# One matrix per system in place of attention and inverse, by factors per row stored with the systems

## The chip, the cores and the metric

The kernel runs on one core of one Trainium2 chip, in fp32. The metric is the device time of one execution in microseconds. Before the change it is 774.7 us, the median of 3 runs (774.45 to 776.15).

## The reference

A small vision tower over 64 images of 96 x 96: patch embedding to 37 tokens of width 256 per image, a first layer (multi-query attention and a mixture by entmax gates), a second layer, then 8 experts with top-1 routing. The change is in the second layer's attention, a gated delta rule. An image has 37 tokens, fewer than one chunk of 64, so the state stays zero and what remains is, per image and head (2 heads of 128):

```python
k = x / max(norm(x), 1e-12)                    # x: normalised rows, one head
v = (x @ W_write.T) * beta;  beta = sigmoid(x @ W_beta.T)
A0 = tril(-(k*beta) @ k.T * L, -1)             # L[i, j] = gamma ** (i - j)
A = solve_triangular(eye - A0, eye, lower=True, unit_diagonal=True)
attn = tril(k @ k.T * L)
o = attn @ (A @ v)
out = rows + o @ W_read.T                      # both heads side by side
logits = layernorm(out) @ Wr + br              # of the experts' router
```

## The kernel before, in words

The 64 images are worked three at a time: a tile is 111 rows (R = 111, 3 images of 37 tokens), 22 tiles (NT) in 11 pairs (PAIRS). The phase in question is one block of five programs that run beside each other and meet in semaphores; each engine takes its own instructions strictly in the order written.

**Steady loop** (`for i in range(-1, PAIRS + 2)`, about 303 to 447 us). Pair i goes through the first layer's mixture (first_products, gate_first, hidden, second_products, gate_second, outputs on TensorE, ScalarE and VectorE). Pair i-1 is normalised (add_outputs, power_rows on GpSimd, normalise, turn_rows). Pair i-2 gets its values and Gram matrices (row_products: x @ W_write, W_beta and k k^T per head in banks 6 and 7); decay_products on VectorE multiplies the Gram bank by two masks, giving the transposed attention attn_t (kept in memory for all tiles) and the system nf. On GpSimd strengths makes beta times the inverse norms, fold brings the three images' columns of a tile together, 37 wide, times strength. GpSimd's order in turn i is strengths(i-2, 0), fold(i-2, 0), power_rows(i-1), strengths(i-2, 1), add_rows(i-1), fold(i-2, 1); at i = PAIRS the spreads of tiles 0 and 1 follow.

**Systems.** SP stores them to n_rows in device memory and loads them with one system (37 x 37) per partition, in three groups: pairs 0 to 4, 5 to 7 and 8 to 10 (GROUPS). With fewer systems than partitions the columns of the inverse are split over 2, 3 or 4 sets. substitution(g) on VectorE solves two rows per step: one product of two SBUF operands (line 1750) and one reduction (line 1757) per part. It is a generator: between the other duties of a turn advance(budget) runs steps up to a budget by estimated cost (SLOTS). The inverse goes by SP through a_rows and comes back as rows (store_inverses, load_inverses). SP's order is: systems of groups 0, 1; inverses of group 0; systems of group 2; inverses of group 1; the 8 MB load of the experts' W1 (line 1350); inverses of group 2; half of W2; the token rows of all 22 tiles (line 1357).

**Read loop** (`for t in range(2, NT + 5)`, to about 526 us), per tile: spread_inverses (GpSimd, line 1898) makes the block matrix of the inverse times beta; solve_values (TensorE, 1457), copy_solved (ScalarE, 1583), attend (1468), copy_attended (1590), read_out with each head in its own half bank (1478). The first head is scaled by its inverse norm on ScalarE (scale_first, 1605) and added on GpSimd (add_first, 1930), the second head scaled and added on VectorE (add_read, 1784) ahead of statistics (1788), aggregate (1790) and variance (1792); power_outputs on GpSimd (1909, 1910), normalise_outputs on ScalarE (1612), turn_outputs (1491), copy_turned (1597), router_logits (1500), keep_logits on VectorE (1798, with the bias). advance continues the substitution; before tile 10 group 1 has to be finished, before tile 16 group 2. Then come the routing (route) and the experts.

The last turn of the steady loop holds the first tiles of the read loop: on TensorE

```python
if i == PAIRS + 1:
    solve_values(0)
row_products(i - 2, 0)
...
if i == PAIRS + 1:
    attend(0)
    solve_values(1)
row_products(i - 2, 1)
```

## Time and profile before

| what | us |
|---|---|
| median of 3 runs (lowest, highest) | 774.7 (774.45, 776.15) |
| the profiled execution | 774.87 |
| its span, first to last instruction | 773.1 |
| busy: TensorE, VectorE, GpSimd, ScalarE | 691.6, 419.6, 292.1, 246.4 |
| mean granted TensorE clock, of full speed | 0.945 |
| embedding and first attention | 0 to 268 |
| gates by entmax | 268 to 303 |
| steady loop | 303 to 447 |
| read loop, up to the last logits | 447 to 526 |
| routing | 526 to 553 |
| experts | 553 to 773 |

A time in a row is the time from the start of the span. Busy time of TensorE says how long matrix products were in its pipeline; their ends are modelled, so the steps of a turn are read from start to start. What an engine waited for stands in square brackets behind its idle time. Where VectorE or TensorE is busy for a whole window, no wait of theirs decides; where none is, the last one's releaser does.

### The profile page before, as it was taken

The numbers are of one execution on the slowest core, as the hardware profiler recorded it, in microseconds if no ns is written. First come the engines' busy times: TensorE is split into PE (matmuls) and PEld (weight loads), VectorE is DVE, ScalarE is ACT, GpSimd is POOL, SyncE is SP. The second block draws the span as 40 slices with busy tenths as digits, with TensorE's granted clock in tenths as the row PEclk, the third lists the DMA queues.
The fourth block names the chain that finished last, engine by engine and source line by source line (L and its number), as shares of the span: only waits on it lengthen the run. The fifth ranks groups of instructions, "written<-read, shape, count | busy, mean of one in ns | idle before, by whom it ended". The sixth has DMA issues, their size and how long they took to land.

```text
span 773.1 us, 13815 instructions
## 1 busy us (share of the span) xinstructions
PE 691.6 (89%) x4632; PEld 518.9 (67%) x4632; DVE 419.6 (54%) x1120; ACT 246.4 (32%) x679; POOL 292.1 (38%) x483
## 2 busy tenths in 40 slices
PE   5899999999997689999999689497999999999994
PEld 3567776676765445999998567374667676766763
DVE  2466677777665466334389999457233323333331
ACT  0122333333333114344444246261122223232231
POOL 2334454544444100255576687360222322222221
PEclk9899999999998779999999899796799999999998
DMA  8311001111100000000101327598211111111110
GB/s 292 137 37 37 20 25 31 37 37 37 37 1 2 1 1 2 1 8 6 40 8 36 41 44 290 210 361 306 56 40 43 49 54 47 58 42 56 47 35 14
DMA packets 25070, 50.73 MB, mean 66 GB/s; under 512 B 15611, under 2 KB 15741, under 8 KB 24363
## 3 DMA queue, kind: packets, MB, share of 16 engines
q1 hardware_dynamic: 21387, 35.36, 14.4%
q0 software_dynamic: 3328, 10.23, 4.4%
q10 hardware_dynamic: 288, 4.27, 1.4%
q8 instruction: 39, 0.64, 0.4%
q14 instruction: 28, 0.23, 0.1%
HBM read 39.99 MB, written 9.86 MB: 64 GB/s over the span
## 4 chain that ended last, share of the span: by engine, by line
PE 45%; DVE 7%; issue 4%; POOL 3%; ACT 0%; POOLq 0%; DVEq 0%; ACTq 0%
PE psum L1199 12%; PE psum L1175 12%; PE psum L1396 4%; PE psum L1408 4%; PE psum L1188 3%; PE psum L1442 2%; DVE work L1750 2%; PE psum L1376 1%; DVE arena_w L1757 1%; PE psum L1386 1%; PE psum L1018 1%; PE psum L1418 1%; POOL work L1909 1%; PE psum L1448 1%; POOL work L1898 1%
## 5 line engine op out<-in xcount | busy, mean ns | idle before, releaser
L1272 ACT ACTIVATE work<-psum,cst 128x128 f32<-128x128 f32 x208 | 56.5, 383 | 144.2 <-PE psum L1188 144.2
L1175 PE MATMUL psum<-arena_w,work 128*128 x208 | 93.7, 593 | 1.0 <-DVE work L1226 1.0
L1199 PE MATMUL psum<-arena_w,work 128*128 x416 | 94.2, 379 | 0.4 <-ACT work L1272 0.4
L1137 POOL DMA_INDIRECT out<-work,row_i x26 | 25.7, 988 | 158.2 <-DVE work L1248 158.2
L1199 PEld LDWEIGHTS psum<-arena_w,work 128*128 128x128 f32 x416 | 77.1, 190 | 10.5 <-issue 1.1
L1235 DVE COPY work<-psum 128x512 f32<-128x512 f32 x52 | 36.0, 692 | 67.5 <-PE psum L1175 67.5
L347 PE MATMUL psum<-arena_w 128*111 128x256 f32 x264 | 63.3, 392 | 4.9 <-DMA arena_w<-in_pack 4.9
L712 POOL TENSOR_TENSOR arena_w<-arena_w,work 101x592 f32<-101x592 f32 x33 | 39.5, 1198 | 71.6 <-DVE work L578 71.6
L1175 PEld LDWEIGHTS psum<-arena_w,work 128*128 128x128 f32 x208 | 37.5, 190 | 38.6 <-issue 38.6
L347 PEld LDWEIGHTS psum<-arena_w 128*111 128x111 f32 x264 | 46.1, 181 | 19.2 <-issue 9.6
L703 POOL TENSOR_TENSOR arena_w<-arena_w 128x296 f32<-128x296 f32 x66 | 44.0, 689 | 21.2 <-DVE arena_w L546 21.2
L1242 DVE TENSOR_TENSOR tokens<-psum,cst 128x256 f32<-128x256 f32 x26 | 11.1, 425 | 73.9 <-PE psum L1199 73.9
L401 PE MATMUL psum<-arena_w 128*37 128x296 f32 x264 | 41.5, 436 | 3.3 <-ACT arena_w L666 3.3
L635 ACT COPY arena_w<-psum 37x592 f32<-37x592 f32 x33 | 25.2, 763 | 57.8 <-PE psum L412 57.8
L558 DVE TENSOR_REDUCE work<-psum 101x16 f32<-101x592 f32 x33 | 25.4, 770 | 24.0 <-PE psum L401 24.0
L1130 POOL DMA_INDIRECT tokens<-x_rows,row_i x26 | 25.4, 978 | 33.1 <-DVE gate_s L1093 25.5
L1396 PE MATMUL psum<-arena_w 128*128 128x222 f32 x176 | 37.6, 357 | 0.0
L412 PEld LDWEIGHTS psum<-cst,arena_w 101*128 101x128 f32 x264 | 26.1, 148 | 16.7 <-POOL arena_w L712 8.6
L433 PE MATMUL psum<-arena_w 37*32 37x74 f32 x1056 | 24.9, 232 | 13.5 <-DVE arena_w L569 12.2
L433 PEld LDWEIGHTS psum<-arena_w 37*32 37x32 f32 x1056 | 19.5, 108 | 24.3 <-issue 24.3
L627 ACT ACTIVATE arena_w<-arena_w 101x592 f32<-101x592 f32 x33 | 23.5, 711 | 37.4 <-DVE arena_w L561 36.4
L1408 PE MATMUL psum<-arena_w 128*128 128x222 f32 x176 | 35.2, 352 | 0.0
(224 smaller groups left out, 1377.6 us busy)
## 6 DMA issues: line engine op xcount, KB each, us to landing
arena_w<-in_w SPq DMA_DIRECT2D x2, 4096.0 KB, 12.7
arena_w<-in_x SPq DMA_DIRECT2D x22, 333.0 KB, 2.9
x_rows<-tokens SPq DMA_DIRECT2D x22, 192.0 KB, 4.0
arena_w<-in_pack ACTq DMA_DIRECT2D x1, 2442.0 KB, 10.8
cst<-in_packc ACTq DMA_DIRECT2D x1, 1727.0 KB, 14.8
arena_w<-in_pack SPq DMA_DIRECT2D x1, 818.5 KB, 7.1
arena_w<-in_pack SPq DMA_DIRECT2D x2, 384.0 KB, 4.3
arena_w<-n_rows SPq DMA_DIRECT2D x8, 85.6 KB, 3.1
```

The costliest lines, as they stand in the source:

```text
L347: mm = nc.tensor.matmul(bank[0][0:R, j * D:(j + 1) * D], xp[j][:, k * R:(k + 1) * R], w_lin[:, k, :], start=(k == 0), stop=(k == PC - 1))
L401: mm = nc.tensor.matmul(bank[4 + f][e * HP:e * HP + TOK, 0:HH * TOK], qt[:, a:a + TOK], kb[p % 2 * 2 + e], start=True, stop=True)
L412: mm = nc.tensor.transpose(turns_bank[:, c * 128:c * 128 + PR], prob[p % 2][:, c * 128:(c + 1) * 128], ident[0:PR, 0:PR])
L433: mm = nc.tensor.matmul(out[32 * b:32 * (b + 1)], vpad[i % 2][:, v0:v0 + 2 * HD], probs[:, :, r0:r0 + TOK], start=(e == 0), stop=(e == 1))
L703: nc.gpsimd.tensor_tensor(kb[p % 2 * 2 + e].rearrange("p (h s) -> p h s", h=HH), kt[:, a:a + TOK].unsqueeze(1).broadcast_to([128, HH, TOK] ...
L712: nc.gpsimd.tensor_tensor(by_head(prob[p % 2], HP), by_head(prob[p % 2], HP), small[p % 2][:, 2 * NH:3 * NH].unsqueeze(2).broadcast_to([PR ...
L1175: mm = nc.tensor.matmul(bank[2 * j + f][:, :], xgt[j][:, k * 128:(k + 1) * 128], arena_w1[:, bass.ds(expert * (2 * FF) + (k * FF + f * 512 ...
L1199: mm = nc.tensor.matmul(bank[7][:, 0:D], ht[j][:, g * 128:(g + 1) * 128], arena_w2[:, bass.ds(expert * (FC * D) + g * D, D)], start=(g == ...
L1235: nc.vector.tensor_copy(hp[j][:, f * 512:(f + 1) * 512], bank[2 * j + f][:, :]).then_inc(h_out[j], 1)
L1272: nc.scalar.activation(ht[j][:, g * 128:(g + 1) * 128], bank[4 + f][:, k * 128:(k + 1) * 128], ACT.Gelu, bias=cst[:, bass.ds(expert * FC + ...
L1396: mm = nc.tensor.matmul(bank[2 + f // 2 % 2][:, (f % 2) * W:(f % 2 + 1) * W], w_out1[:, f, :], z1, start=True, stop=True)
L1408: mm = nc.tensor.matmul(bank[1][:, 0:W], w_in2[:, f, :], hid[:, f * W:(f + 1) * W], start=(f == 0), stop=(f == OC - 1))
```

## The change

One matrix per system takes the place of two. Row i of attn is row i of (M - 1) over beta plus attn's own diagonal, so attn @ A is the inverse with a factor per row plus a diagonal of 1/beta. attn_t, its mask, its product on TensorE and the copy between are dropped. Each row of a system is stored with two more numbers (NW = 39 in place of 37 columns): the diagonal's share and the row's factor. At the end of substitution(g) the solved columns are multiplied by the row's scale, and the diagonal's share (own, one product on GpSimd, own_factors) is added: three more VectorE operations per group in place of none. factors(i) on VectorE makes the two numbers for a pair, a reciprocal and a fused operation on four elements per partition, behind GpSimd's strengths.

Both heads now have the right scale before read_out, which sums them in one bank (bank 2 + t%2): scale_first and add_first are dropped and add_read is one plain addition. The `EPS` addition of the variance goes from VectorE to GpSimd, keep_logits to ScalarE without the bias, which route adds once for all tiles. strengths handles a pair at a time; GpSimd's order becomes power_rows, strengths, fold, fold, add_rows. identity_columns of all groups move into turns 0 to 2 of the steady loop, and the systems of all groups have places of their own. On TensorE the read loop's order becomes attend(t), turn_outputs(t-5), read_out(t-1), router_logits(t-5); on ScalarE copy_attended, copy_turned, normalise_outputs, keep_logits. The diff, cut:

```diff
+NW = TOK + 2
...
+                link(tt(by_tile(lgr), by_tile(lgr), c("b_r", R).unsqueeze(1).broadcast_to([R, NT, NE]), ALU.add))
...
+                    sp.wait_ge(factors_ready, 2 * (t // 2 + 1))
...
-                def solve_values(t):
-                    if not tile(t):
-                        return
-                    pe.wait_ge(a_block, t + 1)
-                    free(pe, vn_out, t - 1)
-                    for h in range(H1):
-                        mm = nc.tensor.matmul(bank[t % 2][0:R, h * 128:(h + 1) * 128], ab[t % 2][:, h * R:(h + 1) * R],
-                                              x_half(t)[:, h * 128:(h + 1) * 128], start=True, stop=True)
-                    mm.then_inc(vn_done, 1)
-
                 def attend(t):
                     if not tile(t):
                         return
-                    pe.wait_ge(vn_out, t + 1)
+                    pe.wait_ge(a_block, t + 1)
                     free(pe, o_out, t - 1)
                     for h in range(H1):
-                        a = (t * H1 + h) * R
-                        mm = nc.tensor.matmul(bank[2 + t % 2][:, h * R:(h + 1) * R], vn[t % 2][:, h * 128:(h + 1) * 128],
-                                              attn_t[:, a:a + R], start=True, stop=True)
+                        mm = nc.tensor.matmul(bank[t % 2][:, h * R:(h + 1) * R], x_half(t)[:, h * 128:(h + 1) * 128],
+                                              ab[t % 2][:, h * R:(h + 1) * R], start=True, stop=True)
                     mm.then_inc(o_done, 1)
 
...
-                        mm = nc.tensor.matmul(bank[4 + t % 2][0:R, h * D:(h + 1) * D], ot[t % 2][:, h * R:(h + 1) * R],
-                                              w_read[:, h, :], start=True, stop=True)
+                        mm = nc.tensor.matmul(bank[2 + t % 2][0:R, 0:D], ot[t % 2][:, h * R:(h + 1) * R],
+                                              w_read[:, h, :], start=(h == 0), stop=(h == H1 - 1))
...
                     if i == PAIRS + 1:
-                        solve_values(0)
+                        attend(0)
                     row_products(i - 2, 0)
                     outputs(i - 1)
                     hidden(i, range(OC // 2))
                     if i == PAIRS + 1:
-                        attend(0)
-                        solve_values(1)
+                        attend(1)
+                        read_out(0)
                     row_products(i - 2, 1)
                     gates(i + 1)
                     hidden(i, range(OC // 2, OC))
                     turn_rows(i - 1)
-                pe.wait_ge(y_added, PAIRS)
-                read_out(0)
-                attend(1)
                 for t in range(2, NT + 5):
-                    solve_values(t)
+                    attend(t)
+                    turn_outputs(t - 5)
                     read_out(t - 1)
-                    turn_outputs(t - 5)
-                    attend(t)
                     router_logits(t - 5)
                 route_products(pe)
                 expert_products(pe)
@@ -1575,35 +1553,25 @@
                                          scale=0.5).then_inc(beta_out, 1)
                     nc.scalar.copy(x_half(t), bank[6][0:R, 0:D]).then_inc(v_out, 1)
 
...
                 for t in range(2, NT + 5):
+                    copy_attended(t)
+                    copy_turned(t - 5)
                     normalise_outputs(t - 4)
-                    copy_solved(t)
-                    copy_turned(t - 5)
-                    scale_first(t - 1)
-                    copy_attended(t)
+                    keep_logits(t - 5)
...
-                    nc.vector.tensor_tensor(attn_t[:, t * H1 * R:(t + 1) * H1 * R], bank[7][0:R, 0:H1 * R], lt, ALU.mult)
...
-                    nc.vector.engine_nop().then_inc(solved[g], 1)
+                    nc.vector.tensor_tensor(x, x, n[:, :, TOK + 1].unsqueeze(1).broadcast_to([used, cols, TOK]),
+                                            ALU.mult).then_inc(scaled[g], 1)
+                    dve.wait_ge(scaled[g], 1)
+                    dve.wait_ge(factored[g], 1)
+                    band = rows_x[0:used, 0:(cols - 1) * (TOK + sets)].rearrange("p (c i) -> p c i", c=cols - 1)[:, :, 0:sets]
+                    nc.vector.tensor_tensor(band, band, own[0:used, 0:TOK - 1].rearrange("p (c k) -> p c k", k=sets),
+                                            ALU.add).then_inc(solved[g], 1)
+                    corner = rows_x[0:used, cols * TOK - 1:cols * TOK]
+                    nc.vector.tensor_tensor(corner, corner, own[0:used, TOK - 1:TOK], ALU.add).then_inc(solved[g], 1)
...
-                    dve.wait_ge(inverted, t // 2 + 1)
-                    dve.wait_ge(half_added, t + 1)
-                    nc.vector.scalar_tensor_tensor(h, bank[4 + j][0:R, D:2 * D], inv_all[:, t * H1 + 1:t * H1 + 2], h,
-                                                   ALU.mult, ALU.add).then_inc(added, 1)
+                    dve.wait_ge(summed, t // 2 + 1)
+                    nc.vector.tensor_tensor(h, h, bank[2 + j][0:R, 0:D], ALU.add).then_inc(added, 1)
...
+                def factors(i):
+
+                    if not pair_of(i):
+                        return
+                    cols = slice(2 * H1 * i, 2 * H1 * (i + 1))
+                    b0 = 2 * i % NB
+                    to = nk_all.rearrange("p (b h n) -> p b h n", b=NB, h=H1)[:, b0:b0 + 2]
+                    dve.wait_ge(strong, i + 1)
+                    dve.wait_ge(inv_out, i + 1)
+                    for b in (b0, b0 + 1):
+                        free(dve, n_stored[b], 16 * len(ROW_CUTS) * (2 * i // NB))
+                    nc.vector.reciprocal(to[:, :, :, TOK], beta[:, cols].rearrange("p (b h) -> p b h", b=2)
+                                         ).then_inc(factors_ready, 1)
+                    dve.wait_ge(factors_ready, 2 * i + 1)
+                    nc.vector.scalar_tensor_tensor(to[:, :, :, TOK + 1], sn[:, cols].rearrange("p (b h) -> p b h", b=2), 0.5,
+                                                   to[:, :, :, TOK], ALU.mult, ALU.subtract).then_inc(factors_ready, 1)
...
+                def strengths(i):
+
+                    if not pair_of(i):
+                        return
+                    cols = slice(2 * H1 * i, 2 * H1 * (i + 1))
+                    pool.wait_ge(inverted, i + 1)
+                    pool.wait_ge(beta_out, 2 * i + 2)
+                    link(ts(beta[:, cols], th[:, cols], 1.0, 2e-9, ALU.add, ALU.max))
+                    tt(beta[:, cols], beta[:, cols], inv_all[:, cols], ALU.mult).then_inc(strong, 1)
+                    pool.wait_ge(strong, i + 1)
                     link(tt(strength[:, cols], beta[:, cols], inv_all[:, cols], ALU.mult))
-                    tt(beta_img[:, t * H1 * IPT:(t + 1) * H1 * IPT].rearrange("p (h m) -> p h m", m=IPT),
-                       beta[:, cols].unsqueeze(2).broadcast_to([R, H1, IPT]),
-                       c("mask_img", R).unsqueeze(1).broadcast_to([R, H1, IPT]), ALU.mult).then_inc(beta_masked, 1)
+                    tt(beta_img[:, cols.start * IPT:cols.stop * IPT].rearrange("p (h m) -> p h m", m=IPT),
+                       beta[:, cols].unsqueeze(2).broadcast_to([R, 2 * H1, IPT]),
...
+                def own_factors(g):
+
+                    used = group_of(g)[3] * SETS[g]
+                    pool.wait_ge(zeroed[g], 3)
+                    pool.wait_ge(n_in[g], 16 * H1 * SETS[g])
+                    tt(solve_at[g][3][0:used, :], solve_at[g][2][0:used, :],
+                       solve_at[g][0][0:used, :].rearrange("p (i j) -> p i j", i=TOK)[:, :, TOK], ALU.mult).then_inc(factored[g], 1)
...
-                    pool.wait_ge(vare2, t + 1)
+                    pool.wait_ge(aggr2, t + 1)
                     free(pool, normed2, t - 1)
+                    link(ts(ve2[t % 2][:, 0:1], st2[t % 2][:, 7:8], EPS, None, ALU.add))
...
-                    strengths(i - 2, 0)
+                    power_rows(i - 1)
+                    strengths(i - 2)
                     fold(i - 2, 0)
-                    power_rows(i - 1)
-                    strengths(i - 2, 1)
+                    fold(i - 2, 1)
                     add_rows(i - 1)
-                    fold(i - 2, 1)
                     if i == PAIRS:
                         spread_inverses(0)
                         spread_inverses(1)
                     inverses(i - 1)
-
-                def add_first(t):
-                    if not tile(t):
-                        return
-                    pool.wait_ge(half_out, t + 1)
-                    pool.wait_ge(summed, t // 2 + 1)
-                    tt(h_rows(t), h_rows(t), first_half[t % 2], ALU.add).then_inc(half_added, 1)
-
+                    if i - 3 in ends:
+                        own_factors(ends[i - 3])
                 for t in range(NT + 2):
-                    add_first(t - 1)
                     spread_inverses(t + 2)
                     power_outputs(t - 2)
+                    if t == 4:
+                        own_factors(LAST)
                 send_and_gather(pool)
 
 
@@ -1990,9 +1979,7 @@
```

## Rows read from the trace of the kernel before

**Rows 1.** Windows: us, busy of TensorE, weight loads, VectorE, ScalarE, GpSimd; clock, DMA, GB/s

```profile
397.00:409.00 12.00, 12.00 (x67) 11.00 (x66) 11.54 (x37) 5.15 (x18) 7.71 (x20) 1.00 0.03 5
418.50:440.00 21.50, 14.27 (x80) 12.24 (x78) 20.56 (x55) 6.13 (x22) 14.27 (x34) 0.98 0.27 48
...
470.00:487.00 17.00, 16.85 (x116) 14.27 (x116) 16.24 (x69) 11.79 (x33) 13.72 (x25) 1.00 1.00 410
487.00:500.00 13.00, 2.08 (x15) 1.67 (x14) 4.87 (x17) 1.16 (x4) 0.86 (x2) 0.75 0.43 144
```

**Rows 2.** Timeline of SP's queue: start us, us, engine, line, operation, out<-in, count

```profile
470.66 0.36 SPq L1350 DMA_DIRECT2D arena_w<-in_w  x1
492.13 3.68 SPq L1325 DMA_DIRECT2D a_rows<-arena_w  x8
497.15 2.66 SPq L1331 DMA_DIRECT2D arena_w<-a_rows  x6
...
500.28 27.38 SPq L1357 DMA_DIRECT2D x_rows<-tokens  x44
```

**Rows 3.** Timeline of GpSimd at tile 16

```profile
499.14 0.56 POOL L1898 TENSOR_TENSOR work<-arena_w 111x222 f32<-111x222 f32 x1 [12.39 <-DMA arena_w<-a_rows]
```

**Rows 4.** Timeline of TensorE, one read turn

```profile
506.63 0.67 PE L1457 MATMUL psum<-tokens,work 111*111 111x128 f32 x4
507.14 1.03 PE L1478 MATMUL psum<-cst,work 128*111 128x256 f32 x4
...
508.20 0.61 PE L1468 MATMUL psum<-arena_w,work 111*128 111x111 f32 x4
508.80 0.56 PE L1500 MATMUL psum<-cst,work 128*111 128x8 f32 x4
```

**Rows 5.** Timeline of VectorE, the last tile's first mask

```profile
447.30 0.39 DVE L1696 TENSOR_TENSOR arena_w<-psum,arena_w 111x222 f32<-111x222 f32 x1 [1.23 <-PE psum L1448]
```

**Rows 6.** Timeline of VectorE in the routing

```profile
529.29 0.29 DVE L1046 RECIPROCAL work<-work 111x22 f32<-111x22 f32 x1
```

**Rows 7.** Timeline of VectorE, identity columns of the last group

```profile
443.15 0.53 DVE L1707 TENSOR_TENSOR arena_w<-cst,arena_w 128x370 f32<-128x370 f32 x1
```

**Rows 8.** Timeline of GpSimd, turn PAIRS of the steady loop

```profile
436.84 0.20 POOL L1872 TENSOR_SCALAR arena_w<-arena_w 111x2 f32<-111x2 f32 x1
...
437.95 1.09 POOL L1855 TENSOR_TENSOR tokens<-tokens,arena_w 111x512 f32<-111x512 f32 x1
...
440.12 0.56 POOL L1898 TENSOR_TENSOR work<-arena_w 111x222 f32<-111x222 f32 x1
```

**Rows 9.** Timeline of TensorE, start of the steady loop's last turn

```profile
440.73 1.19 PE L1457 MATMUL psum<-tokens,work 111*111 111x128 f32 x4 [2.42 <-POOL work L1898]
```

**Rows 10.** Timeline of VectorE, one read turn

```profile
464.27 0.48 DVE L1784 SCALAR_TENSOR_TENSOR tokens<-psum,arena_w,tokens 111x256 f32<-111x256 f32 x1
...
465.25 0.18 DVE L1790 BATCH_NORM_AGGREGATE work<-work 111x2 f32<-111x6 f32 x1
465.47 0.15 DVE L1792 TENSOR_SCALAR work<-work 111x1 f32<-111x1 f32 x1
465.54 0.16 DVE L1798 TENSOR_TENSOR work<-psum,cst 111x8 f32<-111x8 f32 x1
```

**Rows 11.** Groups of 303 to 531 us: busy us, mean ns of one | idle before, releaser

```profile
L1930 POOL TENSOR_TENSOR tokens<-tokens,work 111x256 f32<-111x256 f32 x22 | 14.3, 648 | 8.8 <-ACT work L1605 8.7
...
L1909 POOL TENSOR_TENSOR work<-work 111x1 f32<-111x1 f32 x22 | 14.1, 641 | 4.1 <-DVE work L1792 4.1
```

**Rows 12.** Windows of line 1750, then of line 1757: VectorE busy, clock, DMA, GB/s

```profile
462.00:492.00 30.00, 8.36 (x29) 1.00 0.76 294
...
462.00:492.00 30.00, 7.32 (x29) 1.00 0.76 294
```

**Rows 13.** DMA issues of 499 to 516 us: count, KB each, median us to landing

```profile
x_rows<-tokens SPq DMA_DIRECT2D x11, 192.0 KB, 11.1
```

**Rows 14.** Timeline of TensorE in the drain

```profile
520.11 0.56 PE L1500 MATMUL psum<-cst,work 128*111 128x8 f32 x4 [0.43 <-ACT work L1597]
```

More of the change, by code:

```diff
@@ L146, in build @@
         lg0 = carve_1b(NT * E0, R)
+        carve_2 = carver(arena_w1)
+        for g in range(1, len(GROUPS) - 1):
+            solve_at[g] = [carve_2(w) for w in (TOK * NW, TOK * COLS[g], TOK, TOK)]
         zeros = arena_w2[:, W2S - RW // 2:W2S]
@@ L922, in build @@
             ab = [wc(H1 * R, R) for _ in range(2)]
-            vn = [wc(D, R) for _ in range(2)]
             ot = [wc(H1 * R) for _ in range(2)]
@@ L927, in build @@
             halves = wc(4, R)
-            first_half = [wc(D, R) for _ in range(2)]
-            ac = arena_w2[0:R, W2S // 2 + NT * H1 * R:W2S // 2 + NT * H1 * (R + TOK)]
             def pair_of(i):
@@ L1812, in _ @@
                     decay_products(i - 2, 1)
+                    factors(i - 2)
                     if i - 3 in ends:
```

141 lines of the change are left out of this document (56 added, 85 removed).

## The prediction

> **What bounds the kernel now.** I read the windows by stage first [rows 1]. Up to 418 us TensorE is the bound: from 397 to 409 it is busy 12.00 of 12.00 us, VectorE 11.54. From there to 492 us VectorE is: 20.56 of 21.50 us, later 16.24 of 17.00. Between 487 and 500 nobody is: TensorE works 2.08 of 13 us. The experts behind 553 us are TensorE's, and the change doesn't touch them. So it can act in three places: the turn of the pipeline into the read loop (418 to 450 us), the read turns beside the substitution (450 to 492), and the last turns with the routing (500 to 553).
>
> Then the timelines, for what ends each. When VectorE has solved the last group of systems, SP issues its stores at 492.13 and its loads at 497.15 [rows 2]; GpSimd spreads tile 16 at 499.14, after 12.39 us idle that a DMA ended [rows 3]. That chain sets when the last six tiles can start. Behind it a turn takes 2.57 us, and TensorE fills it [rows 4].
>
> **The change, part by part. The steady loop (to 418 us): nothing.** VectorE loses one mask of two per tile (0.39 us alone [rows 5], about 0.3 from start to start) and gains two four-element factor operations per pair. No four-element reciprocal is in the trace: the 22-element one takes 0.29 us [rows 6], the smallest vector operations 0.15, and the second waits for the first. So a pair of factors costs 0.3 to 0.6 us; I take 0.45, towards the reciprocal's row. Minus 0.60 plus 0.45 a pair is covered by a TensorE without a gap; should the factors' wait hold VectorE (11.54 of 12.00 here), each 0.1 us over the 0.46 left is a gap on TensorE in each of some three turns. The exponentials and products dropped ahead of the loop, and the identity columns moved into its first turns, where VectorE is far from full, count zero too.
>
> **The end of the first group (430 us): +1.05.** A substitution gets three operations at its end. A product of 370 elements takes 0.53 us [rows 7], one of 222 the 0.39 of rows 5: a slope of 0.95 ns per element, so the scalings of 703, 481 and 370 elements cost about 0.86, 0.64 and 0.53 us, the band and corner additions 0.15 to 0.20 each. With waits 1.2, 0.95 and 0.85 us. GpSimd's factor product is ready long before. The first 1.2 stands in front of gate_second of the last pair, for which TensorE's outputs wait; the dropped masks and new factors give 0.15 back. Queued behind it on VectorE is the whole last pair.
>
> **The turn into the read loop: +1.35 more.** GpSimd's order changes. Before, strengths and fold of the first tile stand ahead of power_rows; the second tile's strengths start at 436.84, the row addition at 437.95, and with a fold between tile 0's spread starts at 440.12 [rows 8]. After, the strengths (1.1 us, as from 436.84 to 437.95), both folds (1.15 each) and the addition (1.05) all follow power_rows, which ends at about 437.5: 437.5 + 1.1 + 2.3 + 1.1 = 442.0. TensorE waits for this spread ahead of the last pair's row products: it waited 2.42 us, to 440.73 [rows 9], and now waits to about 442.7. In front of the second tile's products stands now a read_out as well (0.87 us, 1.4 while the clock is low), and a product set fewer. The last tile's mask, at 447.30 after a 1.23 us wait for TensorE [rows 5], comes at about 449.6, and the factors behind it wait for strengths that need the same tile's values: another 0.3. The last group's identity columns (0.53) no longer lie in the way, but VectorE waits there anyway. In all the first read addition comes +2.4 us (bounds +0.5, if GpSimd catches up, and +4).
>
> **The read turns on VectorE: -4.0.** One turn is in [rows 10]: the fused read addition takes 0.48 us at 464.27, aggregate 465.25, variance 465.47, logits 465.54. The plain addition of 256 elements should take 0.42 to 0.43 by the mask's 0.39 for 222: 0.05 saved. The variance operation, now GpSimd's, saves 0.19 with its wait, the logits copy, now ScalarE's, 0.07. That is 0.24 in each of 14 turns and 0.07 in nine of them: 4.0. The ends of groups 1 and 2 take 0.95 and 0.85. So the last group is solved at +2.4 - 4.0 + 1.8 = +0.2 us. GpSimd also loses its addition of 0.65 us per turn [rows 11]. The substitution's product (two SBUF inputs) and reduction (one) of equal size take 8.36 and 7.32 us in 462 to 492 [rows 12]: 1.0 us goes there beside a working GpSimd, of which I give back 0.3.
>
> The Trainium skill (SBUF — State Buffer, Who interferes with whom) has it that a VectorE instruction with two SBUF inputs and a GpSimd one that reads SBUF exclude each other. This trace agrees in that only the two-input form is longer; by the page each new scaling, two-input itself, could also be held by one GpSimd operation.
>
> **The queue is a floor.** Group 1 is solved about 2.4 us later too, so the 8 MB weight load, issued at 470.66 [rows 2], goes at about 473. At the 410 GB/s of the window 470 to 487 [rows 1] it takes 20 us: to 493 instead of 491. The last group's stores stand behind it on the same queue: token stores behind the next weight load landed 11 us after their issue [rows 13], which is what such a place costs. Eight stores take 3.68 us to issue, so behind 493 they land at about 497, as now. Solving the last group sooner gains nothing below that. I take 0 for all up to the spread of tile 16, bounds -1 and +2.
>
> The Trainium skill (DMA: Bandwidth & Descriptors, Queues, rings and completion order) says each DMA engine takes a ring's descriptors in order; that would be this floor's reason.
>
> **The last turns: -4.0.** TensorE's turn, by starts: solve 0.51, read and transposes 1.06, attend with the wait for ScalarE's copy 0.60, logits 0.41 [rows 4]. After: attend alone 0.44 (0.51 times 111/128 columns), 1.06, now covering the copy, and 0.41: 1.91. GpSimd's turn is the spread 0.56, an added operation 0.27, the power 0.64 and its follower 0.27 [rows 3, 8, 11]: 1.74, just below. Six turns: -4.0. The turn with the last read has no solve; there the covered copy saves 0.6. In the four turns of drain (logits wait 0.43 for the copy [rows 14], 1.24 a turn at the high clock) the normalisation (0.6) now stands behind that copy and ahead of the next transposes: 1.5 in place of 1.24 in two or three, +0.6. The token stores take 27.4 us of SP from 500.28 [rows 2]; they can end no later than now, and the routing's need for them comes some 8 us after the last logits.
>
> **Routing: +0.4.** The bias is added in one linked operation of 176 elements (0.35, between 0.15 and the mask's 0.39) behind the last logits.
>
> **Sum.** 0.0 - 4.0 + 0.4 = -3.6 on the profiled execution's 774.87 (span 773.1): 771.2. The runs' median, 774.7, is 0.2 lower, less than the terms are good for.
>
> **Rivals.** (A) The turn costs nothing net: GpSimd, with fewer operations per pair, is ahead there, the spread comes by 441 us, and the weight load moves forward with the substitution. For it: GpSimd's row shows no long idle time to lose. Against it: both folds now stand ahead of the spread. Price: VectorE's -2.2 come through, -6: 769. Chance 0.17.
> (B) The last turns don't reach 1.91 us because GpSimd's turn with its waits, or the round over the engines, is 2.25. For it: 1.74 against 1.91 is close. The gain there halves: -1.6, 773.3. Chance 0.15.
> (C) Slower. Tile 0's spread, and TensorE's last row products with it, come later than I say. Each microsecond past 442 delays the last pair's systems, VectorE and the weight load alike: from 445.6 the gain is gone, at 447.5 it is +1.8: 776.7. For it: these are stores and loads of short rows through memory, whose issue moves 1 us. Against it: the spread followed GpSimd's work without idle time, so the loads had landed. Chance 0.09.
> (D) It does not do what it says: the removed chain (solve, copy, second scaling) was hidden, and the two sides cancel: 774.7. It holds for the 14 turns that are VectorE's, not for the last six. Chance 0.04.
>
> **How the numbers follow.** Forecast 0.55 (own range 769.7 to 772.9), A 0.17, B 0.15, C 0.09, D 0.04. The range takes in most of A, B and D: 767.8 to 774.8. A measurement here tells about 0.2%, 1.55 us: faster are the forecast, A and a third of B, less the forecast's upper end, 0.75; same two thirds of B, D and some of the forecast, 0.16; slower C, 0.09.
>
> **What would show it.** Right: tile 0's spread near 442; SP's stores of the last group within 1 us of 492.13 and the 8 MB load near 473; turns of 1.9 us behind tile 16's spread. Wrong: gaps on TensorE before 418 behind factors that wait for strengths; GpSimd full in the last turns; tile 16's spread over 2 us from 499.14.

## The result, and the profile after

The changed kernel takes 780.6 us (median of 7 runs, 777.8 to 783.4) against 774.9 of the kernel before: a ratio of 1.0074 with a 95% interval of 1.0051 to 1.0096. I had predicted 771.2, within 767.8 to 774.8. It is slower, and outside the range. The profiled execution took 782.11 us, its span 780.2 (before: 774.87 and 773.1).

First the sections of the span. The steady loop doesn't start at the same time in every profile (the copy that ends the part ahead of it starts between 300.5 and 303.3 us, in kernels of both kinds alike), so all marks below count from that copy, which is the same in both kernels.

| us from that copy | before | after | difference | forecast of the difference |
|---|---|---|---|---|
| the copy itself, from the span's start | 301.49 | 302.95 | +1.46 | 0 |
| stores of group 0's inverses | 128.56 | 130.70 | +2.14 | +1.05 |
| stores of group 1's inverses | 160.91 | 164.82 | +3.91 | |
| issue of the 8 MB of weights | 169.17 | 173.01 | +3.84 | +2.4 |
| stores of the last group's inverses | 190.64 | 191.37 | +0.73 | +0.2 |
| their loads | 195.66 | 198.44 | +2.78 | 0 |
| last logits on TensorE | 223.84 | 228.20 | +4.36 | -4.0 |
| end of the span | 471.61 | 477.25 | +5.64 | -3.6 |

SP's queue after (answers to [rows 2]: start, us, engine, line, operation, count):

```profile
433.65 2.09 SPq L1317 DMA_DIRECT2D a_rows<-arena_w  x4
...
467.77 2.41 SPq L1317 DMA_DIRECT2D a_rows<-arena_w  x6
...
475.96 0.36 SPq L1343 DMA_DIRECT2D arena_w<-in_w  x1
494.32 3.71 SPq L1317 DMA_DIRECT2D a_rows<-arena_w  x8
501.39 2.66 SPq L1323 DMA_DIRECT2D arena_w<-a_rows  x6
```

TensorE in the last turns after (answers to [rows 4]; L1450 is the one product set that is left, L1460 the read):

```profile
488.70 0.47 PE L1482 MATMUL psum<-cst,work 128*111 128x8 f32 x4
504.10 1.20 PE L1450 MATMUL psum<-work,tokens 111*128 111x111 f32 x4 [14.93 <-POOL work L1891]
505.09 0.58 PE L1473 MATMUL psum<-cst,tokens 111*128 111x111 f32 x2
505.46 1.91 PE L1460 MATMUL psum<-cst,work 128*111 128x256 f32 x4
507.17 0.78 PE L1482 MATMUL psum<-cst,work 128*111 128x8 f32 x4
507.80 1.18 PE L1450 MATMUL psum<-work,tokens 111*128 111x111 f32 x4
```

A turn is 3.70 us here and 3.68 in each of the four that follow, where before took 2.57. Yet TensorE has less to do and no gap: most operations take nearly twice their time (the read 1.91 us against 1.03 in rows 4). The clock column goes with it, the third from the right, 0.50 being the lower level, 1.2 GHz, and 1.00 the 2.4 GHz. Windows of before:

```profile
492.00:498.00 6.00, 0.00 (x0) 0.00 (x0) 0.00 (x0) 0.00 (x0) 0.00 (x0) 0.63 0.20 29
...
506.00:510.00 4.00, 4.00 (x31) 3.43 (x30) 1.61 (x7) 3.19 (x10) 2.73 (x6) 1.00 0.94 393
```

and of after:

```profile
506.00:510.00 4.00, 4.00 (x17) 3.42 (x16) 1.14 (x4) 1.67 (x6) 3.14 (x8) 0.50 0.94 401
510.00:516.00 6.00, 6.00 (x25) 5.30 (x24) 2.06 (x6) 1.74 (x6) 2.65 (x7) 0.50 0.95 350
516.00:522.00 6.00, 6.00 (x24) 5.07 (x23) 1.03 (x3) 2.54 (x7) 2.10 (x6) 0.50 0.98 366
522.00:526.00 4.00, 4.00 (x30) 3.67 (x29) 2.31 (x7) 2.26 (x7) 1.71 (x6) 0.92 0.98 346
```

Both kernels fall to half clock in the stall before tile 16. Before is back at full when the second turn starts, 4.3 us after TensorE resumed; after gets it back 18.5 us after, when five of the six turns are over. At full clock the changed turn takes 1.89 us (475.05 to 476.94, before the stall), and 1.91 was forecast:

```profile
475.05 0.68 PE L1450 MATMUL psum<-work,tokens 111*128 111x111 f32 x4
...
476.94 0.68 PE L1450 MATMUL psum<-work,tokens 111*128 111x111 f32 x4
```

The second thing to see is the end of group 0 (VectorE and GpSimd, interleaved by start; L1733 is the scaling, L1738 the band, L1741 the corner, L1837 GpSimd's row addition; the last line is TensorE's first work behind it, which waited 3.40 us for VectorE's gate_second, where it had waited 1.40 before):

```profile
430.77 1.60 DVE L1733 TENSOR_TENSOR arena_w<-arena_w 120x703 f32<-120x703 f32 x1
431.01 2.49 POOL L1837 TENSOR_TENSOR tokens<-tokens,arena_w 111x512 f32<-111x512 f32 x1
432.40 1.16 DVE L1738 TENSOR_TENSOR arena_w<-arena_w 120x36 f32<-120x36 f32 x1
433.48 0.15 DVE L1741 TENSOR_TENSOR arena_w<-arena_w 120x1 f32<-120x1 f32 x1
...
435.97 1.12 PE L1411 MATMUL psum<-arena_w 128*111 128x256 f32 x4 [3.40 <-DVE arena_w L1623]
```

The scaling takes 1.60 us for the 0.86 of my sum, the band 1.16 for 0.20, and GpSimd's addition 2.49 for the 1.09 of [rows 8].

### The profile page after: what moved, and what is told of

Read it like the earlier page. It is cut to its first block, busy times and chain, and to the rows that moved or that the text cites. A ratio compares the mean times of both kernels' runs of the same rounds, so it can differ in the third digit from the quotient of the medians.

```text
span 780.2 us, 13524 instructions
## 1 busy us (share of the span) xinstructions
PE 689.9 (88%) x4544; PEld 518.4 (66%) x4544; DVE 414.2 (53%) x1092; ACT 234.0 (30%) x655; POOL 283.9 (36%) x451
## 4 chain that ended last, share of the span: by engine, by line
PE 48%; DVE 5%; issue 4%; POOL 2%; DMA 0%; ACT 0%; DVEq 0%; POOLq 0%; ACTq 0%
PE psum L1192 12%; PE psum L1168 11%; PE psum L1389 4%; PE psum L1401 4%; PE psum L1181 3%; PE psum L1435 2%; PE psum L1460 2%; PE psum L1369 1%; PE psum L1450 1%; PE psum L1010 1%; PE psum L1379 1%; DVE work L1720 1%; PE psum L1411 1%; PE psum L1441 1%; PE psum L1482 1%
## 5 line engine op out<-in xcount | busy, mean ns | idle before, releaser
L1450 PE MATMUL psum<-work,tokens 111*128 111x111 f32 x88 | 19.0, 352 | 22.8 <-POOL work L1891 22.8
L562 DVE TENSOR_REDUCE work<-psum 101x16 f32<-101x592 f32 x33 | 25.4, 771 | 24.1 <-PE psum L405 24.1
## 6 DMA issues: line engine op xcount, KB each, us to landing
arena_w<-in_w SPq DMA_DIRECT2D x2, 4096.0 KB, 12.7
```

The lines of the kernel that those rows point to most:

```text
L1450: mm = nc.tensor.matmul(bank[t % 2][:, h * R:(h + 1) * R], x_half(t)[:, h * 128:(h + 1) * 128], ab[t % 2][:, h * R:(h + 1) * R], start=Tru ...
```

## Experiments on the clock

Theory 1: the half clock in the last turns, which the long stall brings, costs the time. Rival: the turns are long by a chain of waits. A dummy is a product whose result nobody reads; it only gives TensorE work.

**Dummies in the stall.** Ahead of tile 16, on the changed kernel (fill_start(pe, 16) issues 16 products of 512 columns):

```diff
+                    if t == 16:
+                        pe.wait_ge(v_out, NT)
+                        pe.wait_ge(n_masked, NT)
+                        fill_start(pe, 16)
                     attend(t)
```

> The changed kernel, with 16 dummy matmuls of 512 columns put on TensorE ahead of tile 16's spread row products (into two banks that are free there), so that TensorE works in a part of the 14.93 us in which it stood before tile 16. Theory 1 (the clock: after the long stall the last six turns ran at half clock, 3.68 us each against 1.89 at full clock): the last turns fall to 1.9 to 2.6 us each, and the time falls by 6 to 9 us, to 772 to 775. Theory 2 (the last turns are long by their own chain of waits, and the low clock only goes along with it): the turns stay near 3.7 us and the time stays at 780.6 within 1 us, or rises by what the dummies delay.

Measured: 774.27 us, ratio 0.9988 (0.9976 to 1.0), 6.6 us by the ratios below the changed kernel. The dummies keep the clock at 1.00 through the stall, and the turns take 1.89 to 1.91:

```profile
486.25 13.98 PE L995 MATMUL psum<-cst 128*128 128x512 f32 x32
501.13 0.70 PE L1451 MATMUL psum<-work,tokens 111*128 111x111 f32 x4 [0.90 <-POOL work L1896]
...
503.04 0.68 PE L1451 MATMUL psum<-work,tokens 111*128 111x111 f32 x4
```

From the last group's loads to the last logits it takes 21.05 us instead of 29.76. Of these 8.7 us 1.6 are given back behind the last logits, in the routing. Theory 1 stands.

**The same on the kernel before** (11 dummies of 512 columns, in banks 0 and 2):

> The kernel before with 11 dummy matmuls of 512 columns on TensorE in its stall before tile 16, as the changed kernel got them. In the kernel before TensorE resumed at 499.7 and the granted clock was back at full by 504.1, so only the first two of its last turns were slow. Theory 1 (the clock sets the last turns only where it is low): tile 16's turn is 1 to 2 us shorter, the four after it keep their 2.57 us, and the time falls by 1 to 2.5 us, to 773 to 774. If the steady turns of before also shorten, the clock was at work in them too and the time falls by 3 or more.

774.38 us, 0.9990 (0.9978 to 1.0002). Loads to last logits 26.33 us instead of 28.18, the first turn 2.63 for 4.31, the others still 2.57. So the clock cost before 1.85 us there and after 8.7. With dummies in both, the two kernels are level (0.9988 and 0.9990): the changed one is 5.3 us shorter in the last turns, but its loads come 2.4 us later and it takes 1.6 us more behind the last logits. By these profiles 1.3 us would remain, which the runs don't show.

**A longer stall in the kernel before** (a memset and four linked 512-column products on GpSimd ahead of tile 16's spread):

> The kernel before, with one memset and four chained 512-column products put on GpSimd ahead of tile 16's spread, which lengthens TensorE's stall there from 10.9 us to about 14 to 16. Theory 1 with the clock decided by the length of the stall: the last turns, 2.57 us in the kernel before, run at half clock and take over 3 us, and the time rises by clearly more than the stall: by 7 to 10 us, to 782 to 785. If the stall only delays what follows: the time rises by the delay alone, 3 to 5 us, to 778 to 780.

785.63 us, 1.0129 (1.0098 to 1.016). TensorE stood 16.10 us, 5.2 more than before, and the last logits came 8.7 later: besides the delay itself, the first three turns took 4.55, 4.53 and 4.13 us in place of 4.31, 2.57 and 2.57. The old kernel can be held at half clock too; late in the third turn the clock was back, 12.7 us after the work resumed. The other 1.5 us of the profile came behind the last logits.

**Idle time or work?** Both could explain 18.5 us against 4.3: the changed kernel stands 4 us longer, and its turns hold less work. One kernel has only 4 dummies, at the start of the stall, which leaves TensorE 11.11 us idle; the other has none there, but one of 512 columns in each of the turns 16 to 18:

```diff
                     turn_outputs(t - 5)
+                    if 16 <= t <= 18:
+                        pe.wait_ge(v_out, NT)
+                        pe.wait_ge(n_masked, NT)
+                        fill_start(pe, 1)
```

> The changed kernel with only 4 dummies of 512 columns at the start of the stall (3.4 us at full clock), which leaves TensorE idle for some 11.5 us before tile 16, about as long as in the kernel before (10.91 us), where the clock was back 4.3 us after the work resumed. If the length of the idle time decides how long the clock stays low afterwards: it is back about 4 us after the resumption, one or two turns at 3.68 and the others at 1.89, and the time is 773 to 776. If it doesn't (the smaller work in a turn of the changed kernel keeps it low): five or six turns at 3.68 and 777 to 781.

> The changed kernel with its stall as it was (no dummies there) and one dummy of 512 columns in each of the turns 16, 17 and 18, so that a turn holds more of TensorE's work, as it did in the kernel before (whose clock came back 4.3 us after the work resumed). If too little work in a turn keeps the clock low: it is back within 4 to 8 us of the resumption, and the later turns take 1.89; the time is 775 to 779. If the stall alone decides: the clock stays at half for about 18 us as in the changed kernel, three turns are 1.7 us longer each, and the time is 783 to 787.

The four dummies bring nothing: 781.86 us, 1.0084 (1.0059 to 1.011), a little above the range of either expectation. The three in the turns bring nearly all: 774.76 us, 0.9999 (0.9986 to 1.0012). With 11.11 us idle and the plain turns (windows of that kernel):

```profile
510.00:516.00 6.00, 6.00 (x26) 5.49 (x25) 2.06 (x6) 1.93 (x7) 2.59 (x7) 0.50 0.93 335
516.00:522.00 6.00, 6.00 (x23) 5.07 (x23) 1.67 (x5) 2.23 (x7) 2.34 (x7) 0.50 1.05 392
```

With 14.65 us idle and a dummy in each of three turns:

```profile
506.00:510.00 4.00, 4.00 (x18) 2.96 (x17) 1.03 (x3) 1.22 (x4) 2.20 (x6) 0.74 1.13 483
510.00:516.00 6.00, 6.00 (x41) 5.02 (x40) 2.49 (x8) 2.71 (x10) 3.43 (x9) 1.00 0.85 288
```

TensorE is busy without a gap in both. In the kernel with a dummy a turn its first two dummies (L994) and the second and third turn read:

```profile
504.33 1.94 PE L994 MATMUL psum<-cst 128*128 128x512 f32 x2
...
508.23 0.68 PE L1450 MATMUL psum<-work,tokens 111*128 111x111 f32 x4
...
508.93 1.04 PE L994 MATMUL psum<-cst 128*128 128x512 f32 x2
...
511.00 0.68 PE L1450 MATMUL psum<-work,tokens 111*128 111x111 f32 x4
```

A dummy costs 1.7 us at half clock, and the clock was back 5 us after the work resumed, before the second one started. The second turn, dummy and all, takes 2.77 us, where the plain turn takes 3.68 at half clock; the turns behind the dummies take 1.89.

So here more work in the first turn brought the clock back (5 us for 18.5), and a shorter idle time (11.11 for 14.93 us) did not. That the work which the change took out would have done the same is argued, from the 4.3 us of the kernel before, and not shown: the same old turns, behind 16.10 us idle, were at half clock for 12.7 us. Whether the moment of the first dummy matters beside its work was not tested either.

## Experiments on the solving and the queue

**Without the finishing operations** (with the 16 dummies in the stall, as in all kernels from here on that build on the changed one; the inverses stay unfinished, so this one leaves a part of the work out):

```diff
-                    nc.vector.tensor_tensor(x, x, n[:, :, TOK + 1].unsqueeze(1).broadcast_to([used, cols, TOK]),
-                                            ALU.mult).then_inc(scaled[g], 1)
...
-                    nc.vector.tensor_tensor(band, band, own[0:used, 0:TOK - 1].rearrange("p (c k) -> p c k", k=sets),
-                                            ALU.add).then_inc(solved[g], 1)
...
-                    nc.vector.tensor_tensor(corner, corner, own[0:used, TOK - 1:TOK], ALU.add).then_inc(solved[g], 1)
+                    nc.vector.engine_nop().then_inc(solved[g], 2)
```

> As the changed kernel with the 16 dummies, and the three finishing operations of VectorE on a group's systems (the scaling by the column factors, the band and the corner added) left out, so the stored systems are unfinished: part of the computation is missing. My forecast priced the three at 1.05, 0.95 and 0.85 us at the ends of groups 0, 1 and 2. If they cost what the trace after suggests (the scaling 1.60 us, the band 1.16 and the chain behind them late by 2.0), group 0's and group 1's parts of the chain end about 2 us earlier each, and the time is 2.5 to 4 us below the kernel with dummies alone. If the queue of transfers (8 MB of weights, then the last group's stores and loads) sets the start of the last turns, group 1's end is hidden in part and the time falls by 2 us or less.

770.16 us, 0.9950 (0.9931 to 0.9969): 2.9 us by the ratios below the kernel with dummies alone. By the marks group 0's stores come 2.75 us sooner, group 1's 3.28, the last group's 4.09, but its loads only 3.25. The three operations cost at group 0 2.75 us where I had 1.2; the end of the first group is therefore mis-sized, and the two others add 0.5 and 0.8, where I had 0.95 and 0.85.

**Dense factors.** GpSimd copies the factor of each row into a dense tile beforehand, the scaling reads that:

```diff
-                    nc.vector.tensor_tensor(x, x, n[:, :, TOK + 1].unsqueeze(1).broadcast_to([used, cols, TOK]),
+                    nc.vector.tensor_tensor(x, x, factor[g][0:used, :].unsqueeze(1).broadcast_to([used, cols, TOK]),
```

> The changed kernel with the 16 dummies, and the scaling's second operand, the factors that lie one in each row of 39, copied into a dense tile of 37 by GpSimd beforehand (one small operation a group). The scaling took 0.83 us for 370 columns, 1.40 for 481 and 1.60 for 703, 2.2 to 2.9 ns a column, against 1.2 for the products beside it. If the stride of the operand makes it slow: 0.45 to 0.5, 0.6 to 1.1 and 0.85 to 1.1 us, and the time falls by 0.8 to 1.5 us. If it is GpSimd beside it or the broadcast: durations as they were, and no change within 0.5 us.

The scalings fall from 1.60, 1.15 and 0.84 us (with dummies alone) to 1.04, 0.66 and 0.55:

```profile
430.17 1.04 DVE L1740 TENSOR_TENSOR arena_w<-arena_w,work 120x703 f32<-120x703 f32 x1
431.25 1.15 DVE L1744 TENSOR_TENSOR arena_w<-arena_w 120x36 f32<-120x36 f32 x1
...
492.15 0.55 DVE L1740 TENSOR_TENSOR arena_w<-arena_w,work 128x370 f32<-128x370 f32 x1
```

So the reading with a stride cost a third and more, and 0.55 for 370 elements is close to the 0.53 of [rows 7]. The band stays at 1.15 us: it ended at 432.40, GpSimd's row addition at 432.33. The time doesn't move, 0.9990 (0.9978 to 1.0002); the last group's stores come 0.4 us sooner, its loads 25.28 us behind the weights, as ever.

**The queue.** From the issue of the 8 MB to the last group's loads it is 25.43 us after, 25.33, 25.39 and 25.28 in the three kernels with dummies so far, whatever the solve does, and 26.49 before. First I tried ScalarE's queue for the 8 MB, in its read turn 10:

> The changed kernel with the 16 dummies, and the 8 MB load of the first expert weights issued from ScalarE's queue as soon as group 1's inverses are stored, instead of from SyncE's queue behind group 1's loads (issue at 473.09 in the kernel with dummies). If the queue's order (weights, then the last group's stores and loads behind them) sets the start of tile 16, which my forecast took for hidden and the trace after puts at 2 us, the last group's stores land and its inverses are back 1.5 to 3 us earlier, and the time falls by 1.5 to 3 us below the kernel with dummies alone (ratio 0.995 to 0.997). If the engines share the bandwidth so that the last group's stores wait all the same: within 0.5 us of it.

785.69 us, 1.0132 (1.0112 to 1.0153). The load was issued at 478.06, 2.2 us later by the marks than with the dummies alone, since ScalarE reached the place only then (its copy at 477.84 stands just ahead). The last group's stores were issued from 495.14 on, while the weights still came in (312 GB/s from 495 to 499), and took 8.52 us to issue for 3.71:

```profile
495.14 8.52 SPq L1318 DMA_DIRECT2D a_rows<-arena_w  x8
505.00 2.65 SPq L1324 DMA_DIRECT2D arena_w<-a_rows  x6
```

Why the issue itself was slow is not shown; from 499 to 503.7 the DMA engines were only 0.19 busy. The 16 dummies ended 3.93 us before tile 16's first products, and the clock was lost again: all six turns behind it take about 3.7 us. So this run mixes two losses and says nothing on the order itself. The next does: SP's own order, with 6 MB ahead of the last group and the second weights behind the rows' stores:

```diff
-                sp.dma_start(arena_w1[:, :], w1_h).then_inc(w1_in, 16)
+                sp.dma_start(arena_w1[:, 0:W1A], w1_h[:, 0:W1A]).then_inc(w1_in, 16)
                 store_inverses(LAST)
                 load_inverses(LAST)
-                sp.dma_start(arena_w2[:, 0:W2S // 2], w2_h[:, 0:W2S // 2]).then_inc(w2a_in, 16)
+                sp.dma_start(arena_w1[:, W1A:W1S], w1_h[:, W1A:W1S]).then_inc(w1_in, 16)
                 for t in range(NT):
...
+                sp.dma_start(arena_w2[:, 0:W2S // 2], w2_h[:, 0:W2S // 2]).then_inc(w2a_in, 16)
                 sp.wait_ge(x_stored, 16 * len(ROW_CUTS) * NT)
```

> The changed kernel with the 16 dummies in the stall, and SyncE's transfers in another order: three quarters of the first expert weights (6 MB) where all 8 MB went, the last quarter behind the last group's loads, and the 4 MB of second weights behind the stores of the normalised rows instead of ahead of them. In all four kernels with the 8 MB ahead, the loads of the last group's inverses were issued 25.3 to 25.4 us after the 8 MB (25.43, 25.33, 25.39, 25.28), whether its solve ended 0.5 us earlier or later; before it was 26.5. If the queue sets this: the loads come 5 us behind the stores (6.86 with the 8 MB ahead), no wait for the rows' stores (0.83 us) is left ahead of the routing, and the time falls by 2 to 3 us below the kernel with dummies alone (ratio 0.995 to 0.9965). If the distance between stores and loads is the stores' own time: within 0.5 us of it.

770.68 us, 0.9952 (0.9933 to 0.9971), faster than both kernels and 2.8 us below the dummies alone:

```profile
492.87 3.67 SPq L1319 DMA_DIRECT2D a_rows<-arena_w  x8
497.88 2.66 SPq L1325 DMA_DIRECT2D arena_w<-a_rows  x6
```

5.01 us from stores to loads, as in [rows 2], for 7.07 in the changed kernel. The floor was real, 2.05 us high. The time from issue to landing shows it too (number of transfers, KB each, median us). In the changed kernel:

```profile
a_rows<-arena_w SPq DMA_DIRECT2D x6, 20.8 KB, 3.4
```

and with the new order:

```profile
a_rows<-arena_w SPq DMA_DIRECT2D x6, 20.8 KB, 1.8
```

Stores that take longer behind a running load of their own queue agree with the ring order of the Trainium skill (DMA: Bandwidth & Descriptors, Queues, rings and completion order). The 2.8 us are of two kinds, since two transfers moved: by the marks the loads come 1.7 us sooner, the turns give 0.3 back, and behind the last logits 1.4 are saved, where VectorE no longer waits for the rows' stores (0.83 us with the dummies alone).

**The same on the kernel before:**

> The kernel before with the dummies in the stall and the transfers in the new order, as the counterpart of the changed kernel with the same two (0.9952). In before the stores land without waiting for the weights (5.02 us from stores to loads), so the order should bring it nothing at the last group, and it is at the 0.9990 of its dummies within 0.001; the change would then be worth 0.3 to 0.5% (2.5 to 4 us, my forecast's 3.6) once clock and queue stand the same. If it comes to 0.9955 or less, the change is worth nothing even then.

775.20 us, 1.0000 (0.9978 to 1.0021). Its stores had never waited, and it gains nothing. Against it the changed kernel with the same additions is 0.48% or 3.7 us faster, though the two intervals all but touch, each of the two was compared with other runs of the kernel before, and the changed one scatters: six of its nine runs lie at 769.9 to 770.8 us, three at 774.0 to 775.3. By the profiles: loads +0.45, turns to the last logits -4.92, behind them +0.63, together -3.84.

**Order and dense factors together:**

> The changed kernel with the 16 dummies, the transfers in the new order and the dense factors for the scaling. With the 8 MB ahead, the dense factors shortened the three scalings by 1.5 us together and the time not at all (0.9990 against 0.9988), which the queue explains: the last group's loads came 25.3 us after the weights' issue all the same. With the new order the loads follow the stores at 5.0 us, so if that is the explanation the dense factors are now worth 0.4 to 1.5 us: 769.2 to 770.3, ratio 0.9933 to 0.9947. If they are worth nothing here either, what the scaling takes lies beside other waits in the read turns, and the ratio stays at 0.995.

772.45 us, 0.9975 (0.9955 to 0.9994): not the gain hoped for, and not told from the order alone (0.9952). By the marks the loads come 0.8 us sooner, the last logits 0.6, but its experts start at half clock: their first eight products take 6.21 us for 3.69. TensorE had stood 2.69 us for the gathered rows just ahead, 0.72 in the kernel with the order alone. In each of the three profiles with such a start it had stood 2.69 to 3.74 us there, in the others at most 0.72. Why the rows come late in some executions stays open; it may be what the three slower runs of the order alone had.

**Dummies in drain and routing.**

> The changed kernel with the 16 dummies, and more dummies in the turns that only turn outputs (one of 192 columns in each of the last four), ahead of the router's counting products (3) and ahead of the 44 products of 52 columns (10 where 6 stood). With the dummies in the stall alone the last turns grew from 1.15 to 1.82 us as the clock fell to half, and the 44 products took 9.63 us at half clock against 7.89 in the kernel before, where they began at full clock. If the clock is what gave back 2.9 us between the last logits and the experts: the drain is 1 to 2 us shorter, the 44 products fall to 5 to 8 us, and the time falls by 3 to 5 us below the kernel with the first dummies alone (ratio 0.992 to 0.995). If not, the dummies only delay and the time rises by up to 2.

773.24 us, 0.9978 (0.9959 to 0.9996), 0.8 us below the first dummies and not told from them, not 3 to 5. From the last group's loads to the last logits it took 0.7 us less (20.33 for 21.05) and the 44 products took 8.01 us for 9.63. But VectorE then waited for the stores of the rows, which stand behind the second weights in the queue:

```profile
531.03 0.73 DVE L1065 TENSOR_TENSOR tokens<-work,cst 111x550 f32<-111x550 f32 x1 [2.86 <-DMA x_rows<-tokens]
```

With the first dummies alone this wait was 0.83 us, in the changed kernel none: a gain in the last turns is partly given back here. The wait is gone in the kernel with the new order.

**All of it, on both kernels:**

> All that helped, together on the changed kernel: dummies in the stall, in the last four turns and in the routing, the dense factors for the scaling, and the transfers in the new order. The drain's dummies gained 1.9 us in the turns and then waited 2.86 for the rows' stores; with the stores ahead of the second weights that wait should be gone. Expected by the sum: dummies 6.4 below the changed kernel, the order 2 to 3, drain and routing 2.5 to 4, the dense factors 0.5 to 1.5: 766 to 770 us, ratio 0.988 to 0.993. If it stays at 0.996 or above, something else (the end of the solving, or the weights' transfers ahead of the experts) has become the bound.

> The kernel before with the same additions (dummies in the stall, in the last four turns and in the routing, the transfers in the new order), to see what the change itself is worth when clock and queue are the same for both. My forecast had the change at 3.6 us faster, of it 4.0 in the last turns; with dummies the last turns of the two kernels from tile 16's loads to the last logits took 21.05 and 26.33 us. If the shorter chain of the read turns shows once clock and queue are out of the way, this is 2 to 4 us slower than the changed kernel with all additions; if the longer end of a group's solve eats it, the two are within 1 us.

(The 1.9 us for the drain in the first of these was a misreading; the marks give the 0.7 told above.) 773.66 us, 0.9967 (0.9953 to 0.9980), and 772.67 us, 0.9967 (0.9952 to 0.9983). With the routing's dummies the 44 products of the changed kernel took 6.05 us, but then the gathered rows were waited for 3.04 us and the first experts' products ran at half clock (6.27 us for eight, against 3.69). In this form the two kernels are level, and the dummies in the routing brought nothing that the time shows.

## Why the prediction was wrong, point by point

**The last turns (forecast -4.0).** The structure was right: 1.89 us a turn against my 1.91 at full clock, and 21.05 against 26.33 us from loads to last logits with the clock held in both, -5.3. The step that failed is the silent one, that six turns of after would run at the clock of rows 4. I took the clock of those turns (1.00) as given by the stage, and five of the six ran at 0.50. The front rows had a warning, 0.75 in 487 to 500 [rows 1]; I used it for nothing. Measured: 29.76 us for 28.18, +1.6 in place of -4.0; 8.7 us of the 29.76 were the clock's, against 1.85 in the kernel before.

**The end of the first group (+1.05).** Right in place, mis-sized: 2.14 at the stores, with 2.75 for the three operations instead of 1.2. A third of the scaling was the stride of its factors, which no row of mine had. The other part is the band, 1.16 us for 36 columns beside GpSimd's addition; that of the last group, of 36 columns too, took 0.20 at 494.03 with GpSimd idle. The exclusion of the Trainium skill (SBUF — State Buffer, Who interferes with whom) that I cited and left out of the sum agrees with these rows: the band ended at 433.56, GpSimd's addition at 433.50. I had looked at the scaling alone.

**The turn into the read loop (+1.35 more).** From the copy, tile 0's spread came 2.98 us later (forecast 1.9) and the first read addition 3.6 (forecast 2.4). The order of events was as I told it; both are late by what the step ahead had in excess, and the term itself is 1.46 (3.60 less the 2.14 of the stores) for 1.35. The clock had a hand here as well, which neither I nor a rival had: after the 3.40 us of waiting for gate_second it was at 0.50 from 438 to 450, where before it was at 0.50 to 0.56 from 440 to 446, and the value products at 436.93 took 1.56 us for the 1.04 of before. What that cost in time was not measured.

**The read turns (-4.0, with the ends of two groups +1.8).** From the first read addition to the last group's stores it takes 37.18 us for 40.05: -2.9, forecast -2.2. With this the last group's stores came at +0.73, forecast +0.2.

**The queue (0, bounds -1 and +2).** I named the floor and took its cost for nothing, since I had the weights at +2.4 and my own sum (493, stores landed at 497) left no slack. The loads came at +2.78, outside the bound of +2. By the marks 0.73 of it is the later end of the solving and 2.05 the wait behind the weights. Two things were too small: the weights came at +3.84, not +2.4, and the loads follow their issue by 25.4 us, where my sum had 24 (473 to 497).

**Routing (+0.4).** Right: from the last logits to TensorE's counting products it is 4.10 us for 3.73. Behind them the 44 products take 8.80 for 7.89 us, which no row of mine had: the sections of the span behind the last logits are 1.28 us longer.

**The steady loop (0).** Right: the copy to group 0's stores without its finishing is 0.6 us shorter than before. The four-element reciprocal took 0.17 us, the second factor operation 0.17 as well, so the pair was below my 0.45.

**The rivals.** None of the four had the clock in it. C had the right sign and a part of the mechanism, tile 0's spread past 442 (it came at 444.56, 443.1 less the 1.46 of the start), but by its own price that gives no loss (its 447.5 less 445.6 is also 1.9, not the 1.8 it says). The sum of -3.6 is near what the two kernels differ by once both have dummies and the new order, -3.7; that is in part luck, since the turns gave more (-4.92) and loads and routing took more than forecast, and in two other pairs, with the stall's dummies alone and with all additions, the kernels are level.

## What to carry to other kernels

Before you price a shorter turn of TensorE behind a stall, read the granted clock of the turns that follow, before and after: here fewer products a turn went with half clock for 18.5 us in place of 4.3. Then try a dummy product in the first turn (it cost 1.7 us at half clock, and every turn at full clock was 1.8 us shorter). When small transfers stand behind a large one in a queue, look whether they keep a fixed distance from the issue of the large one (25.3 us here, whenever they themselves were ready); splitting off the part that isn't needed yet freed them. And cost an elementwise operation by a row with the same strides and with the same neighbour on GpSimd, not by its number of elements.

## What the runs showed of the hardware that I had not expected

A TensorE that is busy in every microsecond of a window (6.00 of 6.00) was held at half clock for 18.5 us after it resumed in the changed kernel, and for 22 us in the ones with four dummies and with ScalarE's queue; with one more 512-column product in the first turn it had full clock after 5 us. The plain turns followed idle times of 14.93, 11.11 and 3.93 us, the turn with the dummy 14.65 us; 0.90 us idle behind 16 dummies left the clock full. The old turns got it back after 4 us behind 10.91 us idle and after 12.7 behind 16.10; what makes that difference I can't say. A scaling whose second operand lies 39 elements apart ran at 2.3 to 2.4 ns an element, the dense one at 1.4 to 1.5.
